# The front of the attention heads: x in halves, the first four heads' rows written first, the second batch's projections in one stretch, small pieces between the maxima

## The reference, cut to what matters

```python
x = L0_attn_x                                   # (2, 1024, 128), float32
mod = (silu(L0_c) @ L0_wmod).reshape(2, 6, 1, -1)
h = layernorm(x) * (1 + ca) + sa                # ca, sa from mod
q, k, v = h @ Wq.T, h @ Wk.T, h @ Wv.T          # 16 heads of 8 columns
attn = softmax(q @ k.T / sqrt(8))               # per batch and head, 1024 x 1024
x = x + ga * (attn @ v)
```

## Time and profile before

| | |
|---|---|
| runs, median (lowest, highest) | 1133.54 us (1132.91, 1134.47) |
| profiled execution: time, span | 1135.81 us, 1134.5 us |
| granted TensorE clock, mean | 0.941 of 2.4 GHz |
| busy: TensorE, VectorE, ScalarE, GpSimd | 92%, 85%, 72%, 46% |
| first matmul of a maximum, first score | 30.73 us, 60.94 us |
| last maximum starts | 342.0 us |

### The profile page before, as it was taken

The page is one execution under the profiler, slowest core; times in us unless marked ns, Lnnn a source line. Parts: engine busy times, 40 slices in busy tenths (PEclk is TensorE's granted clock), DMA queues, the critical chain, the costliest instruction groups (busy, mean ns, idle before and its releaser), DMA issues. The chain is left out here.

```text
span 1134.5 us, 21410 instructions
## 1 busy us (share of the span) xinstructions
PE 1043.9 (92%) x7835; PEld 650.8 (57%) x7835; DVE 969.5 (85%) x1327; ACT 818.4 (72%) x1593; POOL 517.9 (46%) x487
## 2 busy tenths in 40 slices
PE   6899999999999887989999999899999996599997
PEld 4222222222222333458988984468888984388896
DVE  6899999999995676979999996989999999866666
ACT  3279898999999544978888854888888833246652
POOL 5400441010101111027889982048999974146663
PEclk9779999999999888799999999899999997699999
DMA  5210100001004420107999980118999977512224
GB/s 158 71 44 15 30 16 17 29 16 31 16 2 76 131 57 2 59 1 191 241 249 226 221 210 3 59 28 191 232 246 230 229 184 259 131 50 64 62 64 126
DMA packets 60313, 121.04 MB, mean 107 GB/s; under 512 B 15471, under 2 KB 28783, under 8 KB 59953
## 3 DMA queue, kind: packets, MB, share of 16 engines
q0 software_dynamic: 15440, 52.66, 23.2%
q1 hardware_dynamic: 43064, 64.82, 18.6%
q10 hardware_dynamic: 1704, 2.20, 0.6%
HBM read 58.02 MB, written 13.19 MB: 63 GB/s over the span
## 5 line engine op out<-in xcount | busy, mean ns | idle before, releaser
L2267 PEld LDWEIGHTS m_pair<-filter_w,delta_x_t 128*128 128x128 f32 x2560 | 294.0, 192 | 43.3 <-issue 43.3
L2267 PE MATMUL m_pair<-filter_w,delta_x_t 128*128 128x112 f32 (+3 forms) x2560 | 298.7, 276 | 9.4 <-DVE h_t L2294 4.1
L570 DVE TENSOR_REDUCE neg_max<-max_ps 128x1 f32<-128x1024 f32 x256 | 293.5, 1214 | 10.8 <-PE max_ps L559 10.5
L686 ACT ACTIVATE exp_scores<-score_k 128x512 f32<-128x512 f32 x512 | 273.9, 599 | 20.7 <-PE score_k L678 13.4
L2243 ACT ACTIVATE decay<-delta,a_log 128x1024 f32<-128x1024 f32 x128 | 145.7, 1142 | 50.0 <-DVE normed L2294 28.7
L559 PE MATMUL max_ps<-k_rows,q_rows 48*128 48x512 bf16 x512 | 166.8, 404 | 7.7 <-DVE neg_max L570 6.5
L2235 ACT ACTIVATE filter_w<-filter,b_t 128x112 f32<-128x112 f32 (+1 forms) x576 | 167.4, 374 | 0.0
L706 PE MATMUL score_k<-exp_scores,v_cols 128*32 128x256 f32 x2048 | 165.1, 396 | 0.0
L678 PE MATMUL score_k<-q_rows,k_rows 51*128 51x512 bf16 x512 | 162.8, 391 | 0.6 <-DMA q_rows<-neg_max_rows 0.6
L579 POOL CAST neg_max_parts<-neg_max 128x16 bf16<-128x16 f32 x16 | 3.1, 196 | 228.8 <-DVE neg_max L570 228.8
L559 PEld LDWEIGHTS max_ps<-k_rows,q_rows 48*128 48x128 bf16 x512 | 30.1, 95 | 120.6 <-DVE neg_max L570 91.9
(11 more groups left out here) (343 smaller groups left out, 1726.9 us busy)
## 6 DMA issues: line engine op xcount, KB each, us to landing
c_row<-c_rows SPq DMA_DIRECT2D x64, 512.0 KB, 6.3
x_inner<-normed POOLq DMA_DIRECT2D x16, 512.0 KB, 6.7
delta_x<-mod_memory POOLq DMA_DIRECT2D x15, 512.0 KB, 8.0
delta_x<-x_inner POOLq DMA_DIRECT2D x15, 512.0 KB, 9.0
x_inner<-h_t POOLq DMA_DIRECT2D x14, 512.0 KB, 6.5
mod_memory<-h_t POOLq DMA_DIRECT2D x14, 512.0 KB, 9.1
mod_memory<-normed POOLq DMA_DIRECT2D x12, 512.0 KB, 9.3
gate_up_all<-in_gate_up_w SPq DMA_DIRECT2D x8, 512.0 KB, 7.5
```

The lines of the kernel that those rows point to most:

```text
L570: ve.tensor_reduce(nm[leg % 2][:, 4 * j + qt:4 * j + qt + 1], mps[:, bank:bank + 2, :].rearrange("p a q -> p (a q)"), AX_X, ALU.max, negat ...
L686: ac.activation(pt[a % 4][:, HEADS[r % 4], :], eps[:, bank, :], ACT.Exp, scale=SC).then_inc(*exped.up())
L2267: mm = pe.matmul(vps[blk][:, lo:hi], self.duT[b][:, c, blk * P:(blk + 1) * P], wf[g % 3][:, lo:hi], start=True, stop=True)
```

## The change

- x comes in three pieces: two halves of the first batch, then, behind the small weights, the second batch. Statistics and roots are taken half by half. The second layer's modulation inputs are loaded after the bfloat16 identity.
- First batch: one tile of parts (q or k of a chunk) at a time on the ring's banks. The middle parts of tiles 1 to 3 are ScalarE's, the low part of the last tile is VectorE's, behind the first half of the second batch's normalizations.
- The parts of heads 0 to 3 are written first and all twelve loads of `load_first` are issued by SP; the other heads' parts are written behind.
- The second batch's transposes and projections follow in one stretch ahead of all maxima; ScalarE copies the projection out and GpSimd subtracts. VectorE takes no part.
- The second layer's columns, the second batch's values and all rows of both modulations are cut in 18 small pieces; one follows each of maxima 2 to 19.
- The negative maxima of the first leg are turned one maximum earlier and sent by two queues, SP and ScalarE, two transfers each.
- The second batch's parts are written after the 22 maxima's entries in SP's queue.

```diff
-            sp.dma_start(self.X[:, b * TB:(b + 1) * TB, :],
-                         A["L0_attn_x"][b].rearrange("(k p) d -> p k d", p=P)).then_inc(*self.in_x[b].up(16))
-            if b == 0:
-                sp.dma_start(self.ident[:], A["k_ident"]).then_inc(*self.in_k.up(16))
+        for half in range(2):
+            lo = half * TB // 2
+            sp.dma_start(self.X[:, lo:lo + TB // 2, :], A["L0_attn_x"][0][lo * P:(lo + TB // 2) * P].rearrange(
+                "(k p) d -> p k d", p=P)).then_inc(*self.in_x[half].up(16))
+        sp.dma_start(self.ident[:], A["k_ident"]).then_inc(*self.in_k.up(16))
...
+        sp.dma_start(self.X[:, TB:NT, :], A["L0_attn_x"][1].rearrange("(k p) d -> p k d", p=P)).then_inc(
+            *self.in_x[2].up(16))
...
         po.tensor_copy(self.silrep[l][:], self.sil[l][:, :, None].to_broadcast([P, NB, P])).then_inc(
             *self.silu_spread.up())
...
-        pe.wait_ge(*self.silu_spread.at())
-        wait_from(pe, *bank.open)
-        pe.matmul(bank.ps[:, 0:hi - lo], self.silrep[l][:, b, :], self.wmod[l][:, lo:hi],
-                  start=True, stop=True).then_inc(bank.full[0], 1)
+        n = hi - lo if j % 2 else (hi - lo) // 2
+        if half == 0:
+            pe.wait_ge(*self.silu_spread.at())
+            wait_from(pe, *bank.open)
+        at = half * n
+        mm = pe.matmul(bank.ps[:, at:at + n], self.silrep[l][:, b, :], self.wmod[l][:, lo + at:lo + at + n],
+                       start=True, stop=True)
+        if at + n < hi - lo:
+            return []
...
+    def pe_mod_cols_half(self, l, half, bank):
...
-                    sp.dma_start(qp[row + KR:row + KM, s, leg % 2, :].rearrange("a (k q) -> a k q", k=4),
-                                 mt[leg % 2][12 * j:12 * j + 12, :]).then_inc(*max_in[leg % 2].up(16))
+            def put_max_turn(leg):
+                for engine, heads in ((sp, (1, 0)), (ac, (3, 2))) if leg == 0 else ((sp, range(4)),):
+                    engine.wait_ge(turn_read.sem, leg + 1)
+                    for j in heads:
+                        s, row = head_rows(leg, j)
+                        engine.dma_start(qp[row + KR:row + KM, s, leg % 2, :].rearrange("a (k q) -> a k q", k=4),
+                                         mt[leg % 2][12 * j:12 * j + 12, :]).then_inc(*max_in[leg % 2].up(16))
...
-            normed = []
-            for b in range(NB):
-                root = self.ln_root(self.X, b * TB, (b + 1) * TB, [self.in_x[b].at()])
-                if b == 0:
-                    self.ve_mod_cols(0, cols_ps)
-                    scaled = self.m_scale
-                    ve.wait_ge(*self.ln_aggr.at())
-                    normed += [self.ve_ln_apply(self.X, t, root) for t in range(TB)]
-                    for l in range(2):
-                        self.po_spread(l)
+            self.ac_load_modulation(1)
+            half = TB // 2
+            roots = [self.ln_root(self.X, i * half, (i + 1) * half, [self.in_x[i].at()]) for i in range(2)]
+            self.po_spread(0)
+            normed = [self.ve_ln_apply(self.X, t, roots[t // half]) for t in range(TB)]
+            self.ve_mod_cols(0, cols_ps)
+            scaled = self.m_scale
...
                 max_score(2 * v + 1)
-                if v == NU + 2:
-                    for m in ring.out():
-                        pe.wait_ge(*m)
+                if v == NU + 1:
+                    pe.wait_ge(*ring.out()[0])
+                    pe.wait_ge(*self.identb_set.at())
                     max_turn(0)
+                    for part in range(3):
+                        sp.wait_ge(*to_dram[0][part].at())
+                    sp.wait_ge(*rows_set.at())
...
+                def ac_part_copy(c, side, bank):
+                    ac.activation(rest[:, side, c * CH:(c + 1) * CH], bank.ps[:], ACT.Copy).then_inc(bank.left[0], 1)
+
+                def po_part_rest(c, side, bank):
+                    cs = slice(c * CH, (c + 1) * CH)
+                    po.wait_ge(*part_hi.at())
+                    po.wait_ge(*bank.left)
+                    po.tensor_tensor(rest[:, side, cs], rest[:, side, cs], p[0][:, side, cs], ALU.subtract).then_inc(
+                        *part_po.up())
...
+                def ve_part_lo(c, side, mid_in):
+                    cs = slice(c * CH, (c + 1) * CH)
+                    ve.wait_ge(*mid_in)
+                    ve.tensor_tensor(p[2][:, side, cs], rest[:, side, cs], p[1][:, side, cs], ALU.subtract).then_inc(
+                        *part_ve.up())
+
+                def sp_parts_out(b, heads, ready):
+                    lo, n = heads.start * HD, len(heads) * HD
+                    for i, marks in enumerate(ready):
+                        for m in marks:
+                            sp.wait_ge(*m)
                         for side in range(2):
-                            sp.dma_start(parts[side, b * H:(b + 1) * H, i],
-                                         p[i][:, side, b * S:(b + 1) * S]).then_inc(*to_dram[b][i].up(16))
-
-                def pe_values(c, bank):
-                    wait_from(pe, *bank.open)
-                    for j in range(4):
+                            sp.dma_start(parts[side, b * H + heads.start:b * H + heads.stop, i],
+                                         p[i][lo:lo + n, side, b * S:(b + 1) * S]).then_inc(*to_dram[b][i].up(16))
...
+                def first_batch_parts():
+                    tiles, rest_in = [(c, side) for c in range(2) for side in range(2)], []
+                    for n, tile in enumerate(tiles):
+                        bank = ring.take()
+                        pe_project(*tile, bank)
+                        ac_part_hi(*tile, bank)
+                        rest_in.append(ve_part_rest(*tile, bank))
+                        if n == 0:
+                            po_part_lo(*tile, ve_part_mid(*tile, rest_in[0]))
+                        if n > 1:
+                            po_part_lo(*tiles[n - 1], ac_part_mid(*tiles[n - 1], rest_in[n - 1]))
+                    ve.wait_ge(*self.ln_aggr.at())
+                    ve_second_batch_normed(range(TB, TB + TB // 2))
+                    ve_part_lo(*tiles[3], ac_part_mid(*tiles[3], rest_in[3]))
...
+                def second_batch_mid():
+                    tile, rest_in = rest_known.pop()
+                    po_part_lo(*tile, ac_part_mid(*tile, rest_in))
+
+                def second_batch_parts(c, side):
+                    bank = ring.take()
+                    pe_project(c, side, bank)
+                    ac_part_hi(c, side, bank)
+                    ac_part_copy(c, side, bank)
+                    rest_in = po_part_rest(c, side, bank)
+                    if rest_known:
+                        second_batch_mid()
+                    rest_known.append(((c, side), rest_in))
...
-                sp_parts_out(0)
-                rows_in[0] = [self.mod_row(0, j) for j in range(4)]
+                sp_parts_out(0, range(4), ((part_hi.at(),), (part_mid.at(), part_ve.at()), (part_po.at(), part_ve.at())))
                 for engine in (sp, ac):
                     engine.wait_ge(*early_rows)
+                first_q = qp[:].rearrange("d s a q -> d s (a q)")
                 for part in range(3):
                     load_first(sp, kp, 1, part)
-                    load_first(ac if part < 2 else sp, qp[:].rearrange("d s a q -> d s (a q)"), 0, part)
+                    load_first(sp, first_q, 0, part)
                 sp_load(0, 1)
-                po.wait_ge(*part_lo.at())
+                sp_parts_out(0, range(4, H), ((), (), ()))
+                turned = lambda c: self.turn(normed, col(1), col(0), (scaled,), done=ht, by=(0, 0, 0, 0), chunks=(c,))
+                turned(2)
+                second_batch_parts(2, 0)
+                turned(3)
+                second_batch_parts(2, 1)
+                for side in range(2):
+                    second_batch_parts(3, side)
+                self.ac_silu_c(1)
+                second_batch_mid()
+                self.po_spread(1)
                 po_value_columns()
-                ve.wait_ge(*self.ln_aggr.at())
-                normed += [self.ve_ln_apply(self.X, t, root) for t in range(TB, NT)]
-                self.turn(normed, col(1), col(0), (scaled,), done=ht, by=(0, 0, 0, 1), chunks=(2, 3))
...
-                ahead(0)
-                project(2)
-                ahead(1)
-                ahead(2)
-                project(3)
-                for c in range(2, NC):
-                    values(c)
...
+                def half_values(c, half):
+                    bank = taken[-1] if half else spare_bank()
+                    pe_values(c, bank, range(2 * half, 2 * half + 2))
+                    if half:
+                        v_ready.append(ac_values(c, bank))
+
+                def half_row(l, j, half):
+                    bank = taken[-1] if half else spare_bank()
+                    rows_in[l] += self.mod_row_half(l, j, half, bank)
+
+                def half_columns(half):
```

(31 more changed lines are left out.)

93 lines of the change are left out of this document (41 added, 52 removed).

## The result

The changed kernel took 1145.01 us (median of 6 runs, 1142.31 to 1146.23); the kernel before, on the same chip, 1134.01 us (1132.57 to 1135.36). The ratio is 1.0095, 95% interval 1.0078 to 1.0113: about 11 us slower. A second set on another chip gave 1.0092 (1.0068 to 1.0115). The forecast was 1129.0 us; rival (c) of the prediction, all pieces at 1.2 GHz, had 6.9 us over the kernel before, and the loss is larger than that. What follows is read from one profiled execution of each kernel.

The account below looks back on a forecast made before the run. VectorE's maxima were taken to set the pace, in and ahead of the rounds. 1.9 + 3.7 + 0.7 - 0.4 - 2.2 + 0.7 = 4.4, rounded to 4.5 us: 1133.5 - 4.5 = 1129.0 us, range 1124.5 to 1132.0.

Parts of the forecast that it names:

- rival (c): All pieces among the maxima run at 1.2 GHz, costing 12.8 us; 6.9 us later, 1140.4 us; chance 0.08.
- Part 3: The 22 maxima ahead of the rounds: 3.7 and 0.7 us saved, 0.4 us lost, 2.2 us paid for slow pieces.
- the term of 2.2 us: Cost of pieces beside the first maxima until the clock comes back after two to five tiles; bounds 1.7 to 3.4 us.
- a slow tile: Maximum with a value piece at 1.2 GHz: 1.84 us on TensorE; with a column piece 2.2 us.
- the cover: At 2.4 GHz a tile's matmuls and half a chunk of values take 0.92 us, hidden under VectorE's 1.17 us maximum.
- Part 1 and 2: The way to q and k parts, then to the first maximum: its matmul at 28.8 us, 1.9 us earlier; bounds 1.0 and 3.0.
- The four normalizations: Second batch's normalizations on VectorE ahead of the last low part: 1.8 us from 17.7 us on.
- The pause ahead of maximum 0: TensorE ends the last projection at about 25.7 us and stands still some 3 us, waiting for the loads.
- the fall of the clock near it: TensorE's clock expected down at 28.8 us, after the pause; granted clock 0.5 somewhere between 27 and 35 us.
- 3.7 and 0.7 us: Savings: 3.7 us from no second-batch projections between the maxima, 0.7 us from no wait at the first score.
- 0.4: Loss of 0.4 us on VectorE from one column copy with two small additions among the maxima.
- Part 4's gain: Start of the rounds, maxima 22 to 27: 0.7 us less lost to the slow clock; bounds 0 and 1.3.

Follow-up runs that it names:

- 2: Changed kernel with every matmul of the value and row pieces issued twice; ratio 1.0232 to the kernel before.
- 3: Changed kernel with all 18 pieces in one block ahead of maximum 0, second silu and its spread early; ratio 1.0059 to the kernel before.
- 8: Changed kernel, columns just ahead of maximum 0, second silu early, other pieces four maxima sooner; ratio 0.9973 with three redundant projections (fillers), without them 1111.4 to 1129.4 us.
- 6: Changed kernel, columns early, second batch's rests on VectorE, values and a filler before maximum 0, rows after maxima 0 to 11: 0.9993; fillers also after 12 to 21: 0.9989.
- 9: Changed kernel with column pieces, then value pieces ahead of maximum 0, row pieces after maxima 0 to 11; ratio 0.9987, with one redundant projection behind the values 0.9983.
- 10: Changed front, layer 0's rows earlier, rests on VectorE, columns, values, one filler before maximum 0, layer 1's rows after maxima 0 to 5, fillers after 6 to 21; ratio 0.9976.
- 4: Changed kernel, layer 0's rows behind the first batch's values, columns and values ahead of maximum 0, layer 1's rows after maxima 0 to 5; ratio 1.0023.
- 7: Kernel before with only layer 1's row matmuls moved, as six pieces after maxima 6 to 11; ratio 1.0052.
- 1: Changed kernel plus three redundant 512-column projections ahead of maximum 0 and a 256-column one after maxima 0 and 1; ratio 1.0091.

## Why the prediction was wrong

**The step that failed** is in Part 3: "tiles 2, 3 and on then fill TensorE without a break, and it comes back after two to five tiles", and with it the term of 2.2 us. Measured from tile 2 to tile 20 it is 38.2 - 21.1 = 17.1 us. The clock stayed at 0.50 from 32 to 83 us, of which TensorE was busy without a break from 32 to 70 us, and in 2 with twice the work. I had read the coming-back behind 66 to 68 us of unbroken work as a rule for any unbroken work. The trace of before has a second one, which seemed to bear me out, in the modulation rows ahead of maximum 0:

```profile
26.00:28.00 2.00, 2.00 (x4) 0.96 (x3) 0.71 (x1) 0.91 (x2) 0.00 (x0) 0.50 0.43 146
28.00:30.00 2.00, 2.00 (x12) 1.41 (x11) 0.00 (x0) 1.34 (x4) 0.00 (x0) 0.98 0.47 130
```

So unbroken work brought the clock back in the rounds, in the modulation rows and in the projections (after, 25 us), in the block of 3 only after 9 us, and this loop of maxima and pieces did not do it at all. The nearest stretch of the old trace to it, 42 to 60 us at 0.50 with maxima alone and TensorE 88% busy, I set aside because of the missing 12%. That was a choice, and rival (c), with 0.08, was the one to weigh more.

**A size** was off too: a slow tile costs 2.11 us, not 1.84. From start to start a maximum takes 0.96 us and a piece 1.15 us, where doubling the old trace's durations gave 0.86 and 0.98; what fills the difference, perhaps the switch between the bf16 and the f32 matmuls, was not taken apart. Even at the full clock the cover is thin: in 8 the two take 0.53 + 0.64 = 1.17 us, TensorE busy 18.00 of 18 us, just the 1.17 us of a maximum, where I had counted 0.92. Rival (c) had 12.8 us for all pieces slow; it was 17.1, so even the right rival was 4.3 us short.

**The rest held**, smaller. Part 1 and 2: 1.3 us instead of 1.9, loads as the last wait as said. The four normalizations began at 18.17 us instead of 17.7 and took 2.08 us instead of 1.8, so the low part ended 0.65 us late; SP, whose 5.92 us for six writes hold 1.9 us of waiting for it, passed that on, and the last load landed 1.95 us after its issue, not 2.3. The pause ahead of maximum 0 and the fall of the clock near it came; the pause was 2.0 us instead of 3, since the projections ran partly at 0.50 and ended at 27.4 us, not 25.7. No projection stands between maxima, and the wait at the first score is gone (rows sent at 64.57 us, first score 72.00): 3.7 and 0.7 us, which the slow loop covers and no row shows by themselves. So 1.3 + 3.7 + 0.7 - 0.4 - 17.1 = -11.8 us up to the first score, measured -11.1; 0.7 us stay open. Part 4's gain turned round: the clock came back 11 us after the first score, where before it took 8 us (0.50 to 69 us in its trace).

**The cause, as far as shown.** The loss is the price of the pieces at 1.2 GHz: the traces show the same value and row pieces hidden at 2.4 GHz and 0.94 us each at 1.2. Entered at 2.4 GHz and with no column pieces in it, the loop kept 2.4 GHz in the traces of 6, 8, 9 with the filler, and 10. Where its first piece ran into 1.2 GHz, it stayed there (the changed kernel, 2, 4, the profiled execution of 9 without the filler). 7, entered at 0.50 as well, has projections among its first maxima and was back at 34 us, ahead of its pieces. The columns matter less surely. 1 and 8 with fillers gave 1.0091 and 0.9973, and differ by the columns' place, but also by an earlier second silu and by where fillers and pieces stand. Falls came shortly behind the columns in 1, 4 and the long execution of 9. Against that, the kernel before runs the same twelve column matmuls right ahead of maximum 0 and keeps its clock for 11 us behind them, with projections between its maxima:

```profile
29.40 1.40 PE L256 MATMUL score_k<-silu_c,mod_memory 128*128 128x2 f32 x12
...
30.00:36.00 6.00, 6.00 (x23) 2.70 (x23) 4.42 (x8) 2.99 (x6) 1.45 (x2) 1.00 0.13 38
```

The profiled execution of 8 without fillers kept it too; in 3 it fell before the columns ran, in the changed kernel as they began. So it is not shown that the two-column matmuls bring the clock down; a run with the columns' work replaced by as long a wide matmul in the same place was not made. What the runs do show is that wide fillers behind the columns and ahead of the loop went with short executions: with a filler there, all 10 and all 12 executions were short; without, 2 of 4 and 3 of 12 were long. Why the clock stays down in this loop under a TensorE that is never idle is open. So the change's idea, small pieces under VectorE's maxima, holds at the full clock; what spoiled it was the level of the clock, and with the columns moved and three fillers ahead of the loop the same front gains 3 us.

## What to carry to other kernels

Cost work that is to be hidden beside another engine at both levels of TensorE's clock, and ask at which level the loop is entered: here a value or row piece was free at one and cost 0.94 us at the other, 17 us for the whole loop. Before such a loop put wide matmuls, real ones if there are any, so that TensorE does not wait at its entry: with a redundant filler there every execution was short. The real ones alone, the values in 9, were not enough in 3 of 12. Whether thin matmuls (a few columns) there do harm was not settled. If executions of one kernel fall in two groups, look at the granted clock of each before reading the one profile.

## What the runs showed that I had not expected

- The clock's level can last through a loop: 0.50 over 26 us at 26.00 of 26 us busy, also with every piece doubled (15.00 of 15 us busy, 0.50); but 1.00 over 30 us at 29.60 of 30 when entered at it. It need not last: in 1 the loop was entered at 1.00 and fell.
- Executions of one kernel can fall in two groups: in 9 without the filler 1126.7 to 1133.4 or 1141.0 to 1142.0 us, nothing between, granted clock 0.951 to 0.959 or 0.940 to 0.944; in 7 1116.4 to 1119.7 or 1124.1 to 1127.4 us.
- Beside bf16 maxima of 48 rows, f32 pieces cost 0.96 + 1.15 = 2.11 us at 1.2 GHz, though doubled durations from the old trace gave 1.84.
- x's first half of 256 KB landed only 1.1 us before the old whole (3.95 against 5.07 us), and the second, at 5.81 us, 0.7 us after the old whole.
